# Two selective scans in a four-layer network: step sizes summed on TensorE, softplus in halves, one owned state per half

## The chip, the cores and the metric

The program runs on 1 core of one Trainium2 chip. The metric is the device time of one execution in microseconds (us). It runs ten stages one after the other, with a barrier between them; two of them are the stages that the change touches.

## The reference, cut to what matters

Layers 0 and 3 begin with a Mamba block (a selective scan) whose input is the context and whose gate is the normalised stream. Per batch element (4 of them, 512 time steps, 512 channels, 16 states):

```python
u = silu(conv(in_proj_w @ ctx) + conv_b)
x_dbl = x_proj_w @ u                       # 16 rows of dt_lo, 16 of B, 16 of C
delta = softplus(dt_proj_w @ dt_lo + dt_proj_b)
A = -exp(A_log)
# for each time step t, channel e, state n
state = state * exp(delta * A) + (delta * u) * B_t
y_t = sum_n state * C_t
y = (y + D * u) * silu(z)
```

The other stages (a quantised feed-forward, attentions, two ternary feed-forwards, a routed attention) are the same before and after.

## The kernel before, in words

`stage_mamba` (L294 to L853) is called twice: for layer 0 (stage A here, in the trace from about 60 to 608 us) and for layer 3 (stage B, about 3184 to 3692 us). Channels lie on partitions in EB = 4 blocks of 128, time along the free axis. The work of a batch is NU = 32 units, numbered k = 0 to 31: units 0 to 15 are the 16 states for the first two channel blocks (the first half), units 16 to 31 the same for the other two. A unit n is, across the engines:

- SyncE loads the rows of B and C for the state, spread over 128 partitions (`rows_of`, L416, 5 buffers).
- ScalarE makes two decay tiles dA = exp(delta * A) (L701). There are NA = 3 PSUM banks for them, so it can be at most three tiles, one and a half units, ahead of the scans.
- GpSimd makes dB = du * B for both blocks in one instruction (L733, 4 buffers), and two units later the product of the second block's states with C (L715, `product(n - 2)`).
- VectorE scans the first block (L794), scans the second (L803), and makes the first block's product with C (L811). In an owned unit (`OWN = (5, 12)`, L336, so k = 5, 12, 21, 28) VectorE makes the second product too (L817) and GpSimd skips it.
- TensorE adds both products to y through an identity matrix (L553, L561), a 128x512 matmul in float32 each. The product buffers are 4 deep, so a scan waits for the add of four units before.

Between the units the engines work on the next batch, at places written out by hand (L364 to L372; ScalarE's are three units later, LAG): TensorE's projection (k = 0 to 3), convolution (k = 7 to 10), the small projection (13) and the step sizes (16 to 19); ScalarE's copies, its gates (four silu instructions at k = 10, beside two of the four silu of u; the other two at 13) and Abs and Relu of the step sizes (19 to 22). Stage A also prepares the first batch of stage B, and leaves u, delta and du in DRAM for it (L444), so its four batches all carry such work; of stage B's four batches the last carries none. So there are seven full batches and one bare batch. In stage A's third batch and stage B's first, VectorE also builds the diagonal matrices of layer 3.

Softplus is computed as relu(x) + log(1 + exp(-|x|)) + a correction of the rounding of 1 + exp. Before, over whole 128x2048 tiles:

1. k = 23: ScalarE takes Exp (L655); k = 24: Ln (L659).
2. k = 24: VectorE makes the correction, L765 (two adds of constants) and L766 (a subtraction) (`log_error`).
3. k = 26: GpSimd adds the correction to the logarithm (L709, `add_error`), ahead of its unit's dB.
4. k = 28: VectorE adds the relu (L771) and multiplies by u (L774) (`softplus`), ahead of its unit's scans.

The work on the next batch uses two PSUM banks in turn (`bank`, L403); TensorE waits in `free_bank` until the result that lay in the bank two items before was read.

Of the kernel before, what the change touches and what calls it, by code (L numbers as in the profile page):

```python
# [293 lines left out]
def stage_mamba(chip, name, bc_dram, weights, then=None, given=None):  # L294
# [10 lines left out]
    with ExitStack() as st:  # L305
# [30 lines left out]
        OWN = (5, 12)  # L336
# [18 lines left out]
        s_c, s_err, s_log, s_del, s_du = sem("dve_chain"), sem("log_error"), sem("log"), sem("delta"), sem("du")  # L355
# [10 lines left out]
        SILU, EXP, LOG, ERROR, ADD_ERROR, DELTA = (10, 13), 23, 24, 24, 26, 28  # L366
        LAG = 3
        ROOT, INVERSE = 5, 7

        REWEIGH = {(0, 1): (0, 1), (0, 2): (2, 3)} if given else {(2, 22 + i): (i,) for i in range(4)} if then else {}  # L370
# [7 lines left out]
        if not given:  # L378
            ITEMS += [("project", 0, e) for e in range(EB)] + [("conv", 0, e) for e in range(EB)]
            ITEMS += [("xdbl", 0, 0)] + [("step", 0, e) for e in range(EB)]  # L380
        BEFORE = len(ITEMS)
        AT = {}
        for b in range(B):
            for k in range(NU):
# [4 lines left out]
                if b + 1 < NB:  # L389
                    if k in project_at(b):  # L390
                        here.append(("project", b + 1, project_at(b).index(k)))
                    if k in CONV:
                        here.append(("conv", b + 1, CONV.index(k)))
                    if k == XDBL:
                        here.append(("xdbl", b + 1, 0))
                    if k in STEP:
                        here.append(("step", b + 1, STEP.index(k)))
                AT[b, k] = here
# [8 lines left out]
        def _(sp):  # L407
# [29 lines left out]
            for b in range(NB):  # L437
# [4 lines left out]
                if b == B:  # L442
                    sp.wait_ge(s_du, NB)
# [27 lines left out]
        def _(pe):  # L471
            if given:
                for sem_, count in ((s_x, EB), (s_conv, EB), (s_dbl, 1), (s_dt, EB)):
# [4 lines left out]
            def free_bank(n):  # L478
# [108 lines left out]
        def _(act):  # L587
            act.wait_ge(weights.s_small, weights.SMALL)
            act.activation(a_neg[:], a_in[:], ACT.Exp).then_inc(s_a, 1)
            if given:  # L590
                for sem_, count in ((s_xin, EB), (s_u, EB), (s_dblc, 1), (s_ab, EB), (s_relu, EB), (s_e, 1), (s_ln, 1)):
# [18 lines left out]
            def copy_in(b, e):  # L610
                act.wait_ge(s_x, b * EB + e + 1)
                if b:
                    act.wait_ge(s_err, b)
# [3 lines left out]
            def silu(b, e):  # L617
# [3 lines left out]
                if b >= 2:  # L621
                    act.wait_ge(s_du, b - 1)
# [4 lines left out]
            def gates(b):  # L627
# [3 lines left out]
                for e in range(EB):  # L631
# [11 lines left out]
            def step(b, e):  # L643
                act.wait_ge(s_dt, b * EB + e + 1)
                if b:
                    act.wait_ge(s_del, b)
# [5 lines left out]
            def exp_part(b):  # L652
                act.wait_ge(s_ab, (b + 1) * EB)
                act.wait_ge(s_conv, (b + 1) * EB)
                act.activation(xin[:, :, TAPS - 1:], delta[b % 2][:], ACT.Exp, scale=-1.0).then_inc(s_e, 1)  # L655

            def log_part(b):
                act.wait_ge(s_e, b + 1)
                act.activation(delta[b % 2][:], xin[:, :, TAPS - 1:], ACT.Ln, bias=1.0).then_inc(s_ln, 1)  # L659

            if not given:
# [7 lines left out]
                exp_part(0)  # L669
                log_part(0)  # L670
                norm.root(act)
            for b in range(B):
                act.wait_ge(s_del, b + 1)
                for k in range(NU):
# [4 lines left out]
                    if k == SILU[0]:  # L679
                        gates(b)  # L680
                    for i in REWEIGH.get((b, k - REWEIGH_LAG), ()):
                        reweigh(b, i)
                    if b + 1 < NB:
# [9 lines left out]
                        if k == EXP:  # L693
                            exp_part(b + 1)
                        if k == LOG:
                            log_part(b + 1)
# [8 lines left out]
        def _(pool):  # L705
            def add_error(b):
                pool.wait_ge(s_ln, b + 1)
                pool.wait_ge(s_err, b + 1)
                pool.tensor_tensor(delta[b % 2][:], delta[b % 2][:], du[b % 2][:], ALU.add).then_inc(s_log, 1)  # L709

# [6 lines left out]
            if given:  # L717
                pool.sem_inc(s_log, 1)
            else:
                add_error(0)  # L720
            for b in range(B):
                for k in range(NU):
                    if b + 1 < NB:
                        if k == ADD_ERROR:
                            add_error(b + 1)
                    n, h = b * NU + k, k // N
                    pool.wait_ge(s_du, b + 1)
# [13 lines left out]
        def _(dve):  # L741
# [14 lines left out]
            if given:  # L756
                for sem_ in (s_err, s_del, s_du):
                    dve.sem_inc(sem_, 1)
# [3 lines left out]
            def log_error(b):  # L762
                ex, t = xin[:, :, TAPS - 1:], du[b % 2]
                dve.wait_ge(s_e, b + 1)
                ch.step(dve.tensor_scalar(t[:], ex, 1.0, -1.0, ALU.add, ALU.add))  # L765
                dve.tensor_tensor(t[:], ex, t[:], ALU.subtract).then_inc(s_err, 1)  # L766
# [52 lines left out]
            if not given:  # L819
                log_error(0)  # L820
                norm.inverse(dve)
                softplus(0)
            for b in range(B):
                for k in range(NU):
# [11 lines left out]
                    if b + 1 < NB:  # L836
                        if k == ERROR:
                            log_error(b + 1)
                        if k == DELTA:
                            softplus(b + 1)  # L840
# [2229 lines left out]
```

## Time and profile before

| | |
|---|---|
| median of 3 runs | 4228.2 us (4226.68 to 4228.35) |
| profiled execution | 4224.04 us, of which the traced span 4222.2 us |
| busy over the span: TensorE / VectorE / ScalarE / GpSimd | 85% / 70% / 42% / 36% |
| VectorE's first scan of the first batch, stage A | starts at 90.36 us |
| last gated product's last add, stage A | ends at 607.6 us |
| VectorE's first scan of the first batch, stage B | starts at 3195.66 us |
| last add, stage B | ends at 3692.0 us |

Shares over the whole span say little here, since the stages have different limits. The two stages in question take about 1045 us of the 4222 us. They are read batch by batch, and within one batch unit by unit. In the rows below L-numbers are lines of the kernel before; "idle before" in square brackets is how long the engine had been idle when the instruction started, and what it waited for. Start-to-start distances of the same instruction are what a unit costs; single durations overlap by about 0.1 us. A float32 matmul shows as two records.

### The profile page before, as it was taken

How to read it: one execution, taken by the hardware profiler on the slowest of the kernel's cores; microseconds unless marked ns; L12 is line 12 of the kernel's file. 1: busy time of each engine (PE TensorE's matmuls, PEld its weight loads, DVE VectorE, ACT ScalarE, POOL GpSimd, SP SyncE). 2: the span in 40 equal slices, each digit the busy share in tenths (PEclk: the TensorE clock that was granted, in tenths of full speed). 3: DMA queues.
4: the chain of work that ended last, by engine and by line, in shares of the span. 5: the costliest groups of instructions: out<-in, count | busy, mean ns of one | idle time of the engine just before them, and what ended most of it. 6: DMA issues, size and time to landing. Idle time of an engine off the chain costs nothing. (4 is left out here: it accounts for less than half of the span.)

```text
span 4222.2 us, 46653 instructions
## 1 busy us (share of the span) xinstructions
PE 3601.3 (85%) x15115; PEld 1721.6 (41%) x15163; DVE 2957.5 (70%) x4169; ACT 1763.2 (42%) x2945; POOL 1503.5 (36%) x1038
## 2 busy tenths in 40 slices
PE   5788764999999999898999879785877887689898
PEld 2233322555555555442333344333333332244454
DVE  4889988588777884457888266527667899844663
ACT  3555541222222221243777453327664555421254
POOL 2999863122211220054000100004436999800122
PEclk7899887999999999997999989896998888889999
DMA  3455441121333212366774110001005455412420
GB/s 106 131 144 140 122 139 54 49 80 59 94 101 99 73 34 76 116 144 99 80 79 49 53 60 0 3 8 65 0 0 143 135 138 133 127 47 69 79 54 22
DMA packets 249831, 338.33 MB, mean 80 GB/s; under 512 B 45603, under 2 KB 147523, under 8 KB 248037
## 3 DMA queue, kind: packets, MB, share of 16 engines
q1 hardware_dynamic: 249620, 335.70, 32.0%
q8 instruction: 110, 1.80, 0.2%
q14 instruction: 101, 0.82, 0.1%
HBM read 284.38 MB, written 53.35 MB: 80 GB/s over the span
## 5 line engine op out<-in xcount | busy, mean ns | idle before, releaser
L701 ACT ACTIVATE m_dA<-m_delta,m_a_neg 128x512 f32<-128x512 f32 x512 | 349.9, 689 | 473.3 <-DVE m_H_bank L794 386.5
L553 PE MATMUL m_y<-m_H,ident 128*128 128x512 f32 x512 | 307.3, 689 | 180.0 <-DVE m_H L811 179.9
L1899 DVE TENSOR_REDUCE a_core_minus_max<-a_core_a 128x1 f32<-128x512 f32 x512 | 317.1, 683 | 57.6 <-PE a_core_a L1725 57.6
L733 POOL TENSOR_TENSOR m_dB<-m_du,m_BC 128x1024 f32<-128x1024 f32 x128 | 315.6, 2466 | 44.5 <-DMA m_BC<-bc_ready 33.3
L561 PE MATMUL m_y<-m_H,ident 128*128 128x512 f32 x512 | 298.3, 674 | 34.7 <-POOL m_H L715 34.7
L715 POOL TENSOR_TENSOR m_H<-m_H,m_BC 128x512 f32<-128x512 f32 x224 | 300.1, 1340 | 45.3 <-DVE m_H L803 45.2
L1851 ACT ACTIVATE X<-a_core_s 128x512 f32<-128x512 f32 x512 | 264.6, 603 | 93.1 <-PE a_core_s L1725 93.0
L733 POOL TENSOR_TENSOR XN<-m_du,m_BC 128x1024 f32<-128x1024 f32 x128 | 300.9, 2356 | 2.7 <-DMA m_BC<-bc_ready 2.7
L1291 POOL TENSOR_TENSOR ctxT<-ctxT,f_scales 128x1024 f32<-128x1024 f32 x48 | 105.9, 2206 | 532.8 <-DVE ctxT L1116 532.8
L1357 DVE SCALAR_TENSOR_TENSOR XN<-f_u,f_power_back,XN 128x512 f32<-128x512 f32 x128 | 95.8, 748 | 232.2 <-PE f_u L1188 232.2
L1251 ACT ACTIVATE XN<-f_g,f_power_back 128x512 f32<-128x512 f32 x128 | 88.0, 687 | 404.2 <-PE f_g L1188 404.2
L553 PEld LDWEIGHTS m_y<-m_H,ident 128*128 128x128 f32 x512 | 98.0, 212 | 366.8 <-DVE m_H L811 311.4
L1262 ACT CAST f_inter_high<-XN 128x512 fp32r<-128x512 f32 x128 | 79.5, 621 | 384.5 <-DVE XN L1357 384.5
L1725 PE MATMUL a_core_a<-a_core_k,a_core_q 96*128 96x512 bf16 x512 | 209.2, 411 | 23.6 <-ACT a_core_max_rows L1869 10.1
L1178 PE MATMUL f_acc<-f_wdown_high,f_inter_high 128*128 128x512 f32 x512 | 224.1, 438 | 0.0
L1299 POOL TENSOR_TENSOR XN<-f_mag,ctxT 128x1024 f32<-128x1024 f32 x48 | 127.9, 2664 | 213.4 <-DVE f_mag L1125 107.4
L1180 PE MATMUL f_acc<-f_wdown_high,f_inter_low 128*128 128x512 f32 x512 | 202.7, 396 | 0.0
L1179 PE MATMUL f_acc<-f_wdown_low,f_inter_high 128*128 128x512 f32 x512 | 202.2, 395 | 0.0
L1186 PE MATMUL f_g<-f_xn_high,f_wh 128*128 128x512 f16 x512 | 196.5, 384 | 1.4 <-ACT f_wh L1164 1.4
L1725 PE MATMUL a_core_s<-a_core_q,a_core_k 98*128 98x512 bf16 x512 | 192.0, 386 | 6.0 <-ACT X L1851 4.5
L794 DVE TENSOR_TENSOR_SCAN m_H_bank<-m_dA,XN 128x512 f32<-128x512 f32 x128 | 157.4, 1230 | 56.2 <-ACT m_dA L701 36.6
L1186 PE MATMUL f_u<-f_xn_high,f_wh 128*128 128x512 f16 x512 | 195.0, 381 | 1.4 <-ACT f_wh L1164 1.4
(411 smaller groups left out, 8352.7 us busy)
## 6 DMA issues: line engine op xcount, KB each, us to landing
m_BC<-bc_rows SPq DMA_DIRECT2D x224, 512.0 KB, 4.8
XN<-in_L_ffn_w_dram SPq DMA_DIRECT2D x72, 256.0 KB, 2.7
m_BC<-bc_ready SPq DMA_DIRECT2D x32, 512.0 KB, 5.0
ternary<-ctxT SPq DMA_DIRECT2D x96, 128.0 KB, 1.7
a_core_q<-a_q_parts SPq DMA_DIRECT2D x48, 256.0 KB, 12.8
a_core_k<-a_k_parts SPq DMA_DIRECT2D x48, 256.0 KB, 14.6
f_w_tern<-ternary SPq DMA_DIRECT2D x24, 512.0 KB, 5.9
f_core_q<-f_q_parts SPq DMA_DIRECT2D x24, 512.0 KB, 8.2
```

The lines of the kernel that those rows point to most:

```text
L553: pe.matmul(ps_y[:, 0, :], ident[:], HD[n % NH], start=False, stop=True, skip_group_check=True).then_inc(s_ad, 1)
L561: pe.matmul(ps_y[:, 1, :], ident[:], HP[n % NH], start=False, stop=True, skip_group_check=True).then_inc(s_ap, 1)
L701: act.activation(dA[:, i % NA, :], delta[b % 2][:, e, :], ACT.Exp, scale=a_neg[:, e, k % N:k % N + 1]).then_inc(s_dA, 1)
L715: pool.tensor_tensor(HP[n % NH], HP[n % NH], BC[n % NS][:, 1, :], ALU.mult).then_inc(s_hp, 1)
L733: pool.tensor_tensor(dB[n % ND][:], du[b % 2][:, h * EH:(h + 1) * EH, :], BC[n % NS][:, 0:1, :].broadcast_to([P, EH, L]), ALU.mult).then_i ...
L1178: pe.matmul(ps_acc[:, t, :], high, DH[gb][:, q % 4, :], start=(q % 4 == 0), stop=False)
L1179: pe.matmul(ps_acc[:, t, :], high, DL[gb][:, q % 4, :], start=False, stop=False)
L1180: m = pe.matmul(ps_acc[:, t, :], low, DH[gb][:, q % 4, :], start=False, stop=(q % 4 == 3))
L1186: pe.matmul(out, w[0], xh[:, k, toks], start=(k == 0), stop=False)
L1725: pe_last = pe.matmul(out[:, cols], lhs(c, k), rhs(c, k), start=(c == 0), stop=(c == NCH - 1 and mask is None))
L1851: act.activation(prob[pair][e][:, j, q0:], ps_s[:, at % NR, q0:], ACT.Exp, scale=hs.scale).then_inc(s_exp, 1)
L1899: dve.tensor_reduce(mx[u % 2][:, qt, h:h + 1], ps_a[:, at % NR, 0:n], AX.X, ALU.max, negate=True).then_inc(s_red, 1)
```

## The change

- Softplus goes through in two halves of two channel blocks. Exp of the first half on ScalarE at k = 21, of the second at 22; Ln at 22 and 23. VectorE's correction (the same two instructions, on 128x1024) at k = 22 and 24.
- `add_error` on GpSimd and `softplus` on VectorE go. TensorE sums the three terms of each block through the identity matrix into a PSUM bank (new item "sum", three float32 matmuls of 128x512, at k = 23, 24, 26, 27).
- Two units later VectorE multiplies the block's sum, read from PSUM, by u (`times_u`, four 128x512 instructions at k = 25, 26, 28, 29). Four units after the sum ScalarE copies it to delta (`copy_sum`, four 128x512 copies at k = 27, 28, 30, 31), after `times_u` of the block.
- The gates are split: two at k = 10 and two at k = 13.
- `OWN = (9,)`: one state per half, so k = 9 and 25, is finished by VectorE alone, where there were two.
- The turning of layer 3's weights in stage A moves from k = 22 to 25 to k = 20, 21, 22, 25. GpSimd waits per half for du. In stage A the parking of u, delta and du waits for the last copy.

```diff
-        OWN = (5, 12)
+        OWN = (9,)
...
-        SILU, EXP, LOG, ERROR, ADD_ERROR, DELTA = (10, 13), 23, 24, 24, 26, 28
-        LAG = 3
+        SILU, EXP, LOG, ERROR, SUM = (10, 13), (21, 22), (22, 23), (22, 24), (23, 24, 26, 27)
+        LAG, TIMES_U, COPY_SUM = 3, 2, 4
...
+                elif kind == "sum":
+                    pe.wait_ge(s_del, b * EB + i + 1)
+                    pe.wait_ge(s_du, b * EB + i + 1)
...
+                elif kind == "sum":
+                    pe.wait_ge(s_relu, b * EB + i + 1)
+                    pe.wait_ge(s_ln, 2 * b + i // EH + 1)
+                    pe.wait_ge(s_err, 2 * b + i // EH + 1)
+                    pe.matmul(out, ident[:], delta[b % 2][:, i, :], start=True, stop=False)
+                    pe.matmul(out, ident[:], du[b % 2][:, i, :], start=False, stop=False)
+                    pe.matmul(out, ident[:], positive[:, i, :], start=False, stop=True).then_inc(s_sum, 1)
...
-            def gates(b):
+            def gates(b, h):
...
-                for e in range(EB):
+                for e in range(h * EH, (h + 1) * EH):
...
+            def exp_part(b, h):
+                rows = slice(h * EH, (h + 1) * EH)
+                act.wait_ge(s_ab, b * EB + (h + 1) * EH)
...
+            def log_part(b, h):
+                rows = slice(h * EH, (h + 1) * EH)
+                act.wait_ge(s_e, 2 * b + h + 1)
...
+            def copy_sum(b, e):
+                act.wait_ge(s_sum, b * EB + e + 1)
+                act.wait_ge(s_du, b * EB + e + 1)
+                act.copy(delta[b % 2][:, e, :], bank("sum", b, e)).then_inc(s_del, 1)
...
-            def add_error(b):
-                pool.wait_ge(s_ln, b + 1)
-                pool.wait_ge(s_err, b + 1)
-                pool.tensor_tensor(delta[b % 2][:], delta[b % 2][:], du[b % 2][:], ALU.add).then_inc(s_log, 1)
...
-                    pool.wait_ge(s_du, b + 1)
+                    pool.wait_ge(s_du, b * EB + (h + 1) * EH)
...
-            def softplus(b):
-                dve.wait_ge(s_log, b + 1)
-                dve.wait_ge(s_relu, (b + 1) * EB)
-                dve.tensor_tensor(delta[b % 2][:], delta[b % 2][:], positive, ALU.add).then_inc(s_del, 1)
-                dve.wait_ge(s_del, b + 1)
-                dve.wait_ge(s_u, (b + 1) * EB)
-                dve.tensor_tensor(du[b % 2][:], delta[b % 2][:], u[b % 2][:], ALU.mult).then_inc(s_du, 1)
+            def log_error(b, h):
+                rows = slice(h * EH, (h + 1) * EH)
+                ex, t = xin[:, rows, TAPS - 1:], du[b % 2][:, rows, :]
+                dve.wait_ge(s_e, 2 * b + h + 1)
+                ch.step(dve.tensor_scalar(t, ex, 1.0, -1.0, ALU.add, ALU.add))
+                dve.tensor_tensor(t, ex, t, ALU.subtract).then_inc(s_err, 1)
+
+            def times_u(b, e):
+                dve.wait_ge(s_sum, b * EB + e + 1)
+                dve.wait_ge(s_u, b * EB + e + 1)
+                dve.tensor_tensor(du[b % 2][:, e, :], bank("sum", b, e), u[b % 2][:, e, :], ALU.mult).then_inc(s_du, 1)
```

## Rows read from the trace of the kernel before

**Rows 1.** Busy time by batch, stage B's third and fourth (columns as in the header).

```profile
core 0: us, PE busy (x) PEld busy (x) DVE busy (x) ACT busy (x) POOL busy (x), PEclk, DMA share, GB/s
3453.10:3576.20 123.10, 102.70 (x217) 40.09 (x218) 112.24 (x113) 67.21 (x93) 117.06 (x62) 0.89 0.50 137
3576.20:3685.00 108.80, 76.04 (x153) 28.40 (x153) 101.16 (x108) 47.53 (x67) 105.94 (x60) 0.91 0.53 141
```

**Rows 2.** VectorE in order of time, first scans of k = 10, 18 to 23.

```profile
3491.31 1.23 DVE L794 TENSOR_TENSOR_SCAN m_H_bank<-m_dA,XN 128x512 f32<-128x512 f32 x1 [4.31 <-ACT m_dA L701]
...
3518.28 1.23 DVE L794 TENSOR_TENSOR_SCAN m_H_bank<-m_dA,XN 128x512 f32<-128x512 f32 x1 [0.20 <-DVE m_H L811]
...
3521.71 1.22 DVE L794 TENSOR_TENSOR_SCAN m_H_bank<-m_dA,XN 128x512 f32<-128x512 f32 x1
...
3524.83 1.23 DVE L794 TENSOR_TENSOR_SCAN m_H_bank<-m_dA,m_dB 128x512 f32<-128x512 f32 x1 [0.20 <-DVE m_H L811]
...
3527.95 1.23 DVE L794 TENSOR_TENSOR_SCAN m_H_bank<-m_dA,m_dB 128x512 f32<-128x512 f32 x1 [0.20 <-DVE m_H L811]
...
3532.10 1.23 DVE L794 TENSOR_TENSOR_SCAN m_H_bank<-m_dA,XN 128x512 f32<-128x512 f32 x1
...
3535.22 1.23 DVE L794 TENSOR_TENSOR_SCAN m_H_bank<-m_dA,XN 128x512 f32<-128x512 f32 x1 [0.20 <-POOL m_dB L733]
```

**Rows 3.** VectorE in order of time, k = 24 to 28, around the correction and softplus.

```profile
3541.04 2.29 DVE L766 TENSOR_TENSOR m_du<-m_xin,m_du 128x2048 f32<-128x2048 f32 x1
3543.25 1.22 DVE L794 TENSOR_TENSOR_SCAN m_H_bank<-m_dA,m_dB 128x512 f32<-128x512 f32 x1
...
3550.31 1.23 DVE L794 TENSOR_TENSOR_SCAN m_H_bank<-m_dA,XN 128x512 f32<-128x512 f32 x1 [1.03 <-POOL XN L733]
...
3553.84 1.23 DVE L794 TENSOR_TENSOR_SCAN m_H_bank<-m_dA,XN 128x512 f32<-128x512 f32 x1 [0.61 <-POOL XN L733]
...
3559.53 3.24 DVE L774 TENSOR_TENSOR m_du<-m_delta,m_u 128x2048 f32<-128x2048 f32 x1
3562.69 1.22 DVE L794 TENSOR_TENSOR_SCAN m_H_bank<-m_dA,m_dB 128x512 f32<-128x512 f32 x1
```

**Rows 4.** The correction's first instruction by line: ns min/median/max, first and last start.

```profile
L765 DVE TENSOR_SCALAR m_du<-m_xin x8: 1218/2794/2978, 75.0 to 3538.1; 128x2048 f32<-128x2048 f32 x8
```

**Rows 5.** GpSimd in order of time, same batch.

```profile
3523.41 2.37 POOL L733 TENSOR_TENSOR m_dB<-m_du,m_BC 128x1024 f32<-128x1024 f32 x1
...
3530.49 2.36 POOL L733 TENSOR_TENSOR XN<-m_du,m_BC 128x1024 f32<-128x1024 f32 x1
3532.80 2.35 POOL L733 TENSOR_TENSOR m_dB<-m_du,m_BC 128x1024 f32<-128x1024 f32 x1
...
3538.64 1.27 POOL L715 TENSOR_TENSOR m_H<-m_H,m_BC 128x512 f32<-128x512 f32 x1
3543.47 4.50 POOL L709 TENSOR_TENSOR m_delta<-m_delta,m_du 128x2048 f32<-128x2048 f32 x1 [3.55 <-DVE m_du L766]
...
3557.29 3.32 POOL L715 TENSOR_TENSOR m_H<-m_H,m_BC 128x512 f32<-128x512 f32 x1
3560.58 4.39 POOL L733 TENSOR_TENSOR m_dB<-m_du,m_BC 128x1024 f32<-128x1024 f32 x1
```

**Rows 6.** ScalarE in order of time, same batch, at k = 10 and 24.

```profile
3484.23 2.93 ACT L633 ACTIVATE XN<-X,m_norm_shift,m_norm_rstd 128x512 f32<-128x512 f32 x4
...
3488.53 0.69 ACT L624 ACTIVATE m_u<-m_w,m_small 128x512 f32<-128x512 f32 x1 [0.80 <-PE m_w L524]
...
3534.07 1.28 ACT L659 ACT_TABLE_LOAD   x1
3535.37 1.91 ACT L659 ACTIVATE m_delta<-m_xin 128x2048 f32<-128x2048 f32 x1
```

**Rows 7.** TensorE in order of time, same batch, around the convolution (L524).

```profile
3477.09 1.24 PE L553 MATMUL m_y<-m_H,ident 128*128 128x512 f32 x2 [2.12 <-DVE m_H L811]
3478.12 5.22 PE L524 MATMUL m_w<-m_xin,m_taps 128*128 128x512 f32 x8
...
3484.90 3.60 PE L524 MATMUL m_w<-m_xin,m_taps 128*128 128x512 f32 x8
```

More of the change, by code:

```diff
@@ L365, in stage_mamba @@
         PROJECT, TURN, CONV, XDBL, STEP = (0, 1, 2, 3), (5, 6, 11, 12), (7, 8, 9, 10), 13, (16, 17, 18, 19)
-        SILU, EXP, LOG, ERROR, ADD_ERROR, DELTA = (10, 13), 23, 24, 24, 26, 28
-        LAG = 3
+        SILU, EXP, LOG, ERROR, SUM = (10, 13), (21, 22), (22, 23), (22, 24), (23, 24, 26, 27)
+        LAG, TIMES_U, COPY_SUM = 3, 2, 4
         ROOT, INVERSE = 5, 7
-        REWEIGH = {(0, 1): (0, 1), (0, 2): (2, 3)} if given else {(2, 22 + i): (i,) for i in range(4)} if then else {}
+        REWEIGH = {(0, 1): (0, 1), (0, 2): (2, 3)} if given else {(2, k): (i,) for i, k in enumerate((20, 21, 22, 25))} if then else {}
         REWEIGH_LAG = 1 if given else 3
@@ L379, in stage_mamba @@
             ITEMS += [("project", 0, e) for e in range(EB)] + [("conv", 0, e) for e in range(EB)]
-            ITEMS += [("xdbl", 0, 0)] + [("step", 0, e) for e in range(EB)]
+            ITEMS += [("xdbl", 0, 0)] + [("step", 0, e) for e in range(EB)] + [("sum", 0, e) for e in range(EB)]
         BEFORE = len(ITEMS)
@@ L397, in stage_mamba @@
                         here.append(("step", b + 1, STEP.index(k)))
+                    if k in SUM:
+                        here.append(("sum", b + 1, SUM.index(k)))
                 AT[b, k] = here
@@ L472, in _ @@
             if given:
-                for sem_, count in ((s_x, EB), (s_conv, EB), (s_dbl, 1), (s_dt, EB)):
+                for sem_, count in ((s_x, EB), (s_conv, EB), (s_dbl, 1), (s_dt, EB), (s_sum, EB)):
                     pe.sem_inc(sem_, count)
@@ L668, in _ @@
                     step(0, e)
-                exp_part(0)
-                log_part(0)
+                for h in range(2):
+                    exp_part(0, h)
+                for h in range(2):
+                    log_part(0, h)
                 norm.root(act)
+                for e in range(EB):
+                    copy_sum(0, e)
             for b in range(B):
-                act.wait_ge(s_del, b + 1)
+                act.wait_ge(s_del, (b + 1) * EB)
                 for k in range(NU):
@@ L678, in _ @@
                         act.wait_ge(s_given[k // N], 32)
-                    if k == SILU[0]:
-                        gates(b)
+                    if k in SILU:
+                        gates(b, SILU.index(k))
                     for i in REWEIGH.get((b, k - REWEIGH_LAG), ()):
@@ L692, in _ @@
                             step(b + 1, STEP.index(k - LAG))
[L693 to L696, printed above, removed]
+                        if k in EXP:
+                            exp_part(b + 1, EXP.index(k))
+                        if k in LOG:
+                            log_part(b + 1, LOG.index(k))
+                        if k - COPY_SUM in SUM:
+                            copy_sum(b + 1, SUM.index(k - COPY_SUM))
                     for j in range(EH):
@@ L819, in _ @@
             if not given:
-                log_error(0)
+                for h in range(2):
+                    log_error(0, h)
                 norm.inverse(dve)
-                softplus(0)
+                for e in range(EB):
+                    times_u(0, e)
             for b in range(B):
@@ L836, in _ @@
                     if b + 1 < NB:
[L837 to L840, printed above, removed]
+                        if k in ERROR:
+                            log_error(b + 1, ERROR.index(k))
+                        if k - TIMES_U in SUM:
+                            times_u(b + 1, SUM.index(k - TIMES_U))
                     n = b * NU + k
```

37 lines of the change are left out of this document (11 added, 26 removed).

## Prediction

> **What bounds the kernel now.** I read the two scan stages alone; nothing else is touched. First the busy time by batch [rows 1]: of the 123.1 us of a full batch VectorE is busy 112.2, GpSimd 117.1, TensorE 102.7 (granted clock 0.89 on average). All three are near full, so the next view has to be the order of time. The reader should measure there from first scan to first scan. A plain unit costs VectorE 3.12 us (3521.71 to 3524.83), a unit with one gated product ahead 3.43, so such an extra costs 0.31; an owned unit costs 4.15 (3527.95 to 3532.10) [rows 2]. GpSimd needs 3.54 for a plain unit (two from 3523.41 to 3530.49) and 2.31 for an owned one, since it skips the product [rows 5]. Over 32 units with four owned, VectorE's part is 28 x 3.12 + 4 x 4.15 = 104.0, GpSimd's 28 x 3.54 + 4 x 2.31 = 108.4. VectorE then carries, per full batch, the correction, 8.03 - 3.12 = 4.9 (3535.22 to 3543.25) [rows 2, 3]; softplus, 8.85 - 3.12 = 5.7 (3553.84 to 3562.69); waits of 1.03 + 0.61 for GpSimd right ahead of it [rows 3]; a wait of 4.31 for ScalarE at k = 10 [rows 2]; and eight gated or added products, 8 x 0.31 = 2.5. Each wait replaces a gap of 0.2 that a plain unit has anyway. 104.0 + 4.9 + 5.7 + 1.2 + 4.1 + 2.5 = 122.4 of 123.1: the chain of VectorE explains the batch. GpSimd's 117.1 are inflated: the two operations of softplus stretch its product from 1.27 to 3.32 and its dB from 2.35 to 4.39, and it adds the correction itself, 4.50 after an idle 3.55 [rows 5].
>
> **Part by part, for one full batch.**
>
> *Softplus* goes from VectorE: -5.7. In its place four products that read PSUM, 128x512, of the kind of a gated product: 4 x 0.31 = +1.2. Bounds: +0 (all in existing gaps) to +3.5 (0.68 of work and 0.2 of gap each).
>
> *Owned units* four to two: -2 x (4.15 - 3.12) = -2.1.
>
> *GpSimd's add* goes, and with it VectorE's two waits: -(1.03 + 0.61 - 0.4) = -1.2. GpSimd takes on two products. Its need becomes 30 x 3.54 + 2 x 2.31 = 110.8, plus the time in which VectorE's correction holds it, taken at that correction's free duration, 1.22 + 2.29 = 3.5 [rows 3, 4]: 114.3. That is a floor for a full batch.
>
> *The correction in halves.* L765 takes 1.22 at its fastest, when GpSimd rests, and 2.79 in the median; the one of this batch ran while GpSimd finished a dB and the product of 3538.64, and then L766 took 2.29 unhindered because GpSimd sat idle 3.55 waiting for it [rows 3 to 5]. After the change GpSimd doesn't wait for the correction but goes on, so L766 meets it too, and there are four shorter operations to meet it. Free, the four cost 3.5, less two gaps of 0.28: 3.1. If each waits for a whole dB, 3.1 + 4 x 2.35 = 12.5. I take about 1.1 us of waiting for each, near half of a GpSimd instruction (2.35 or 1.27): 3.1 + 4.4 = 7.5, so +2.6 against 4.9; bounds -1.8 to +7.6.
>
> The Trainium skill (SBUF — State Buffer, "Who interferes with whom") says that a VectorE instruction with two SBUF inputs, or one in a two-port mode, and a GpSimd instruction that reads SBUF exclude each other for the whole instruction, and that whoever issues later blocks. The stretched rows above agree; it speaks for the PSUM operand and against the halves.
>
> *ScalarE at k = 22 and 23.* A switch of function costs a table load of 1.28 [rows 6]; Exp and Ln in halves at different k make four loads where there were two, +2.6. ScalarE's lead is 1.5 units, about 3.75 us, less its two decay tiles. At k = 22 it has Relu and Abs (two like L624's 0.69), Exp and Ln of half the 1.91 of L659 each, and two loads: 5.8 [rows 6]; at k = 23 Ln and two loads, 3.5. The correction's first half on VectorE (3 to 4 us) covers the first, the second half at k = 24 comes too late for the second. I add 0.6 of stall; bounds 0 and 3.5.
>
> The Trainium skill (ScalarE: Activation LUTs, "What ACT_TABLE_LOAD costs") gives 2.66 us for a switch, load and drain together. Here Ln starts 0.02 after the end of its load, so this trace shows 1.28 alone [rows 6].
>
> *Gates split.* At k = 10 ScalarE did two loads, four gates (2.93), two silu: 7.1 us, and waited 0.80 for TensorE's convolution on top [rows 6]; VectorE lost 4.31. Now k = 10 carries 5.5, under cover of the owned unit 9, which adds 1.03 to the lead: stall 0.5 to 1.5. k = 13 carries 5.5 too instead of 3.9, no longer behind an owned unit 12: 5.5 - 3.75 - 0.3 = 1.5. So 2.5 in place of 4.1 (3.2 in stage A): -1.3 on average, bounds -3.5 and +1. The convolution helps: it took 5.22 for the first block at the low clock level (1.2 GHz) after an idle 2.12 that the owned unit 5 had left TensorE, against 3.60 at the high level (2.4 GHz) [rows 7], and unit 5 is no longer owned.
>
> *TensorE* gets 12 matmuls. A convolution block's four take 3.60 at the high level, the last one's tail among it [rows 7], so 0.86 each, 10.3 in all. Its need at that level, 64 adds and 36 other matmuls at 0.86 and 16 transposes of a quarter of that, is 89; with the sums 99 of about 117 us. `times_u` sits two units behind its sum: from the product of unit 22 to k = 25 lie two units and a half correction, about 9 us, against 2.6 for the sum (5.1 at the low level) and 1.7 for two adds. The reuse of a bank waits for `copy_sum`, which ScalarE reaches 1.5 units ahead of VectorE, so before TensorE comes for it; queued behind that wait are the adds, whose buffers are 4 deep. I put +0.5 for it, bounds 0 and +4. The four copies on ScalarE (at most 0.69 each, as L624) hide in its idle time: it is busy 67.2 of 123.1 [rows 1].
>
> *Sum*: -5.7 + 1.2 - 2.1 - 1.2 + 2.6 + 0.6 - 1.3 + 0.5 = -5.4, giving 117.7, above the floor of 114.3. Seven full batches: -38. The bare batch loses two owned units (-2.1) and most of its stall at k = 10, but takes 108.8 now [rows 1] and GpSimd needs 110.8 less a lead of at most 3.5: -1. Before the first batch of stage A the serial chain of the correction, GpSimd's 4.5, and two operations of 2.29 gives way to two sums, a product and copies that end at nearly the same time: -0.8, bounds -3 and +3. At the end of stage A the parking starts some 6 us later, and had 9 us to spare: 0. Layer 3's turning between the sums makes TensorE wait for a copy at k = 25 once: +0.5. Together -39: 4224.0 - 39 = 4185 in the profiled execution. The median of the runs lies 4.2 above that execution; I keep the distance: **4189 us**.
>
> **The rivals.**
>
> *GpSimd sets the pace.* If the corrections hardly meet GpSimd and ScalarE is covered, VectorE's chain falls to about 113 and the floor of 114.3 decides: -8.8 a batch, 7 x 8.8 + 1 = 63, so 4166. For it: GpSimd's 3.54 against 3.12. Against: the measured median of L765.
>
> *The four corrections wait in full.* They cost 12.5 instead of 7.5, the batch falls by 0.4 to 2: 4228 less 3 to 15, about 4218. For it: L765's median, 2.79 against 1.22. Against: the next GpSimd instruction has to be ready each time.
>
> *The table switch costs what the page says.* By the Trainium skill's 2.66 the two more loads cost 2.8 more a batch: 4208. Against: the row above.
>
> *Slower: TensorE at the low clock level.* The sums come exactly where VectorE pauses for the corrections and TensorE idles. From k = 23 to 31 TensorE has 9 x 1.71 + 10.3 = 25.7 us of work at the high level, 51.4 at the low one; VectorE needs 8 x 3.12 + 4.15 + 1.2 + 4.1 = 34.4 and bears a lag of some 3.2. All at the low level costs 51.4 - 37.6 = 13.8 a batch, net +8.4, 59 in all: 4287. It decides from about two thirds of these matmuls at the low level on, where the cost reaches 5.4. For it: the drop in rows 7 after an idle of only 2.12. Against: the second block's 3.60 right behind shows the high level back within some 5 us of steady work, and the sums are steady work.
>
> *It does not do what it says*: the work comes off VectorE but every place it frees is filled by ScalarE's and TensorE's waits: within 8 us of 4228.
>
> **How the numbers follow.** The forecast, 4176 to 4206, 0.58; GpSimd's pace 0.12; full waits of the corrections 0.13, the table switch 0.02; no effect 0.06; TensorE slower 0.09. About 0.2% (8.5 us) is what a measurement can tell. Faster: 0.58 + 0.12 + 0.02 + most of 0.13 = 0.83; same 0.08; slower 0.09. The range leaves out the slower case, half of no effect, and the far end of GpSimd's pace: 4167 to 4222.
>
> **What would show it.** VectorE's pitch over k = 25 to 31 stays 3.12 plus 0.31 where a product with u stands; a wait for TensorE's sum there would break the softplus step. GpSimd's instructions above 3 us vanish, those beside the corrections remain. The halves of L765 and L766 sum to about 7.9 a batch. VectorE's waits for ScalarE are 0.5 to 1.5 at k = 10 and 1.5 at k = 13. TensorE's granted clock from k = 22 to 28 stays mostly high. The prediction is wrong if the batch takes over 121 or under 114 us.

## The result and the profile after

The changed kernel takes 4213.3 us (median of 15 runs) against 4222.7 us for the kernel before (15 runs); the ratio is 0.998, with a 95% interval from 0.9972 to 0.9987. So it is faster by about 9 us, where 39 were forecast. The fifteen runs of the kernel before have a median 5.5 us below that of the three runs from which the forecast started. The time lies inside the range, but the range reached to within a microsecond of 4222.7, so that says little. The profiled execution took 4212.0 us against 4224.0, its span 4210.3 against 4222.2.

Where the 12 us of the span lie, by the first scans of the batches: the start of the first stage costs 3.5 us more (first scan at 93.88 against 90.36 us), stage A's 127 units from first to last first scan take 12.8 us less, stage B's 4.3 us less, and the other stages differ by 1.6. Batch by batch (before, after, in us): stage A 128.7 / 124.1, 123.7 / 123.6, 135.4 / 131.0; stage B 134.4 / 135.7, 123.1 / 121.0, 123.1 / 121.0. The last batch of a stage has no next one to measure to; from its first to its last first scan it is 119.4 / 115.6 in stage A and, the bare batch, 105.8 / 104.4 in stage B. The forecast had wanted 5.4 from each full batch.

Busy time of stage B's third and fourth batch in the changed kernel, which answers to [rows 1] (columns as in its header):

```profile
core 0: us, PE busy (x) PEld busy (x) DVE busy (x) ACT busy (x) POOL busy (x), PEclk, DMA share, GB/s
3442.80:3563.80 121.00, 105.01 (x241) 42.52 (x242) 113.88 (x115) 71.89 (x101) 111.41 (x63) 0.96 0.53 140
3563.80:3671.30 107.50, 75.57 (x153) 25.58 (x154) 99.49 (x106) 50.04 (x69) 107.49 (x62) 0.95 0.53 141
```

GpSimd is down from 117.1 to 111.4, near the need of 110.8 that was forecast, and TensorE's clock is up from 0.89 to 0.96. But VectorE, from which softplus and two owned units had gone (7.8 us by the prediction's terms, with 1.2 us of products coming in), is busy 113.9 of 121.0, 1.6 more than before. The order of time shows on what. VectorE in the third batch of stage B, from the correction ahead of k = 22 to the first product with u, ahead of k = 25, which answers to [rows 3] (L780 and L781 are the correction, L786 the products with u, L806 the first scans):

```profile
3518.12 6.26 DVE L780 TENSOR_SCALAR m_du<-m_xin 128x1024 f32<-128x1024 f32 x1
3524.42 1.23 DVE L781 TENSOR_TENSOR m_du<-m_xin,m_du 128x1024 f32<-128x1024 f32 x1
3525.56 1.23 DVE L806 TENSOR_TENSOR_SCAN m_H_bank<-m_dA,XN 128x512 f32<-128x512 f32 x1
...
3528.67 1.23 DVE L806 TENSOR_TENSOR_SCAN m_H_bank<-m_dA,XN 128x512 f32<-128x512 f32 x1 [0.20 <-ACT m_dA L727]
...
3531.51 1.81 DVE L780 TENSOR_SCALAR m_du<-m_xin 128x1024 f32<-128x1024 f32 x1
3533.35 3.25 DVE L781 TENSOR_TENSOR m_du<-m_xin,m_du 128x1024 f32<-128x1024 f32 x1
3536.53 1.22 DVE L806 TENSOR_TENSOR_SCAN m_H_bank<-m_dA,m_dB 128x512 f32<-128x512 f32 x1
...
3539.36 0.67 DVE L786 TENSOR_TENSOR m_du<-m_w,m_u 128x512 f32<-128x512 f32 x1
```

An instruction with 0.68 us of work (what it takes in stage A's third batch, beside an idle GpSimd) is recorded for 6.26: the recorded time includes a wait. GpSimd at the same time:

```profile
3517.93 2.38 POOL L747 TENSOR_TENSOR XN<-m_du,m_BC 128x1024 f32<-128x1024 f32 x1
3520.23 1.29 POOL L736 TENSOR_TENSOR m_H<-m_H,m_BC 128x512 f32<-128x512 f32 x1
3521.46 2.38 POOL L747 TENSOR_TENSOR m_dB<-m_du,m_BC 128x1024 f32<-128x1024 f32 x1
3527.97 1.27 POOL L736 TENSOR_TENSOR m_H<-m_H,m_BC 128x512 f32<-128x512 f32 x1 [4.13 <-DVE m_H L815]
3529.20 2.34 POOL L747 TENSOR_TENSOR m_dB<-m_du,m_BC 128x1024 f32<-128x1024 f32 x1
3531.51 1.25 POOL L736 TENSOR_TENSOR m_H<-m_H,m_BC 128x512 f32<-128x512 f32 x1
3532.73 2.79 POOL L747 TENSOR_TENSOR XN<-m_du,m_BC 128x1024 f32<-128x1024 f32 x1
```

GpSimd goes through three instructions at full pace, the one in progress when L780 comes (3517.93) and two that begin after it. The third ends at 3523.84; L780 ends 0.54 later, about the time it needs. GpSimd had by then run out of work: its next product waits for a scan that stands behind L780 on VectorE. So VectorE waited until GpSimd was waiting for VectorE. Six of the seven full batches show this (L780 between 6.16 and 7.25), always ended by GpSimd running dry; in the seventh, stage A's third, GpSimd was idle and it took 0.68. At the second half the instruction got in one instruction later (1.81), then L781 waited out a dB (3.25, of which 1.23 is work). Five of the seven second halves are alike to 0.02 us; stage A's third and fourth are cheaper (1.39 and 3.25; 0.68 and 2.17).

### The profile page after: what moved, and what is told of

Its sections match the earlier page's. It is cut to its first block and busy times, and to the rows that moved or that the text cites. A ratio compares the mean times of both kernels' runs of the same rounds, so it can differ in the third digit from the quotient of the medians.

```text
span 4210.3 us, 47286 instructions
## 1 busy us (share of the span) xinstructions
PE 3635.0 (86%) x15355; PEld 1743.4 (41%) x15355; DVE 2959.2 (70%) x4185; ACT 1801.8 (43%) x3009; POOL 1463.2 (35%) x1046
## 5 line engine op out<-in xcount | busy, mean ns | idle before, releaser
L566 PE MATMUL m_y<-m_H,ident 128*128 128x512 f32 x512 | 283.3, 641 | 150.0 <-DVE m_H L823 149.6
L747 POOL TENSOR_TENSOR m_dB<-m_du,m_BC 128x1024 f32<-128x1024 f32 x128 | 302.0, 2360 | 123.0 <-DVE m_du L786 84.5
L574 PE MATMUL m_y<-m_H,ident 128*128 128x512 f32 x512 | 268.4, 612 | 12.0 <-POOL m_H L736 11.9
L1201 PE MATMUL f_u<-f_xn_low,f_wh 128*128 128x512 f16 x512 | 194.8, 380 | 0.0
## 6 DMA issues: line engine op xcount, KB each, us to landing
a_core_q<-a_q_parts SPq DMA_DIRECT2D x48, 256.0 KB, 12.8
```

Source lines behind the costliest of these rows:

```text
L566: pe.matmul(ps_y[:, 0, :], ident[:], HD[n % NH], start=False, stop=True, skip_group_check=True).then_inc(s_ad, 1)
L574: pe.matmul(ps_y[:, 1, :], ident[:], HP[n % NH], start=False, stop=True, skip_group_check=True).then_inc(s_ap, 1)
L747: pool.tensor_tensor(dB[n % ND][:], du[b % 2][:, h * EH:(h + 1) * EH, :], BC[n % NS][:, 0:1, :].broadcast_to([P, EH, L]), ALU.mult).then_i ...
```

## The experiments

"Starves" below means: the VectorE instruction is held through the GpSimd instruction in progress and through others that begin after it. Unless said otherwise the pitches given are of stage B's third batch: "unit k" from its first scan to the next one, with the correction that lies between. So the corrections ahead of k = 22 and 24 lie in units 21 and 23.

**1. The add of constants left out.**

```diff
-                ch.step(dve.tensor_scalar(t, ex, 1.0, -1.0, ALU.add, ALU.add))
-                dve.tensor_tensor(t, ex, t, ALU.subtract).then_inc(s_err, 1)
+                dve.tensor_tensor(t, ex, ex, ALU.subtract).then_inc(s_err, 1)
```

> The changed kernel without the first instruction of each half's correction (the adds of +1 and -1, L780); the second subtracts the exponential from itself, so the rounding correction is left out. Theory (the single-source add starves while GpSimd issues back to back; the two-source subtract gets in at the next boundary): the unit before the first correction falls from 10.28 to 3.12 + at most 2.35 + 1.23 = 6.7 us, the second from 7.86 to about 5.5 to 6.7; a full batch falls from 121.0 by 3 to 6 us, all runs by 20 to 40 us. Rival (the 6.3 us are a wait of VectorE for ScalarE's Exp or a queue behind it, not for GpSimd): the subtract takes over the 6.3 us and the batch falls by at most 1 us.

The result of this kernel lacks the rounding correction. 4189.3 us, 0.992 of the kernel before (0.9904 to 0.9937), batch 117.5. The saving came, but not by the theory. VectorE in this kernel, the first and the second half's remaining instruction:

```profile
3500.07 6.80 DVE L780 TENSOR_TENSOR m_du<-m_xin 128x1024 f32<-128x1024 f32 x1
...
3512.74 2.34 DVE L780 TENSOR_TENSOR m_du<-m_xin 128x1024 f32<-128x1024 f32 x1
```

The two-input instruction starves just as long: 5.57 us of wait and 1.23 of work. The rival's number for the subtract was right, but its cause wasn't: GpSimd's third instruction ends at 3505.78, again where the wait ends. Of the 3.5 us that the batch saves, 2.0 are the second half's second wait and 1.4 the two adds' own work.

**2. No correction at all.**

```diff
-                ch.step(dve.tensor_scalar(t, ex, 1.0, -1.0, ALU.add, ALU.add))
-                dve.tensor_tensor(t, ex, t, ALU.subtract).then_inc(s_err, 1)
+                dve.sem_inc(s_err, 1)
...
-                    pe.matmul(out, ident[:], du[b % 2][:, i, :], start=False, stop=False)
```

> The changed kernel with no correction at all: VectorE's L780 and L781 and TensorE's middle matmul of each sum are left out, so delta lacks the rounding correction. Theory: VectorE loses 11.9 us a full batch, so its chain would be 109.1 us, below GpSimd's 30 x 3.54 + 2 x 2.31 = 110.8 us; the batch lands at 110.8 to 112.5 us and VectorE shows waits of 0.6 us for GpSimd in many units. Time about 4213 - 7 x 9.3 = 4148 us. Rival (TensorE or ScalarE hold the batch): it stays above 116 us.

4157.7 us, 0.9846 (0.9829 to 0.9862), batch 113.5. The correction costs the changed kernel 56 us, 7.5 a batch. The wait that now comes last is not GpSimd's, as I had expected, but ScalarE's: 2.71 at k = 22 and 2.06 at k = 23. There ScalarE changes four times between Ln and the Exp of the decay tiles, a table load each time, and in the changed kernel these loads lay hidden behind the starving instruction. Run 8 tests that.

**3. The add written with two inputs**, to tell whether the kind of instruction decides.

```diff
-                ch.step(dve.tensor_scalar(t, ex, 1.0, -1.0, ALU.add, ALU.add))
+                ones = minus_one[:].rearrange("p (a o) -> p a o", a=1).broadcast_to([P, EH, L])
+                ch.step(dve.scalar_tensor_tensor(out=t, in0=ex, scalar=1.0, in1=ones, op0=ALU.add, op1=ALU.add))
```

> Same arithmetic as the changed kernel, but the first correction instruction is written with two SBUF inputs (exponential + 1, then plus a tile of -1) instead of one. It takes 1.2 us free instead of 0.68. Theory: a two-source instruction gets in at the next GpSimd boundary, so each takes at most 2.35 + 1.2 = 3.6 us, and L780's 6.3 us of the first half fall to 2.5 to 3.6; the second half's rise from 1.8 by up to 1 us. A full batch falls by 1 to 4 us, the kernel by 7 to 28 us. Rival (both kinds starve alike): L780 stays at 6 us or more in the first half, and the kernel becomes 0 to 8 us slower.

The tile `minus_one` is filled once at the start. 4221.8 us, 0.9997 (0.9987 to 1.0006): what the rival said, and 8.6 us slower than the changed kernel. All instances of the line (min, median, max in ns, first and last start):

```profile
L783 DVE SCALAR_TENSOR_TENSOR m_du<-m_xin,m_minus_one x16: 1214/2344/6997, 74.5 to 3541.8; 128x1024 f32<-128x1024 f32 x16
```

In the first half six of the seven wait 4.6 to 5.8 us. The number of inputs does not decide; my theory of the single-source form fell with runs 1 and 3.

**4. GpSimd rests during both corrections.** The arithmetic is unchanged, and nothing but two waits is added.

```diff
+                    if b + 1 < NB and k == ERROR[0] + 1:
+                        pool.wait_ge(s_err, 2 * (b + 1) + 1)
                     pool.wait_ge(s_du, b * EB + (h + 1) * EH)
...
+                    if b + 1 < NB and k == ERROR[1] + 1:
+                        pool.wait_ge(s_err, 2 * (b + 1) + 2)
                     if n >= 2:
                         product(n - 2)
```

> The changed kernel with two waits on GpSimd: at k = 23 its dB waits for the first half's correction, and at k = 25 its product waits for the second half's. GpSimd then rests while VectorE corrects. Theory: the first correction takes 0.7 + 1.2 us (10.28 becomes 5.0 us), the second 0.1 to 0.8 + 1.2 us (7.86 becomes about 5.2 us); GpSimd loses some 2 us twice and its need is 110.8 + 4 = 115 us; a full batch 115 to 117 us, the kernel 4213 - 7 x 5 = 4178 us (4170 to 4190). Rival (the long add is no contention): nothing on VectorE shrinks, and GpSimd's rest costs up to 4 us a batch: 4213 to 4240 us.

4178.4 us, 0.9893 (0.9877 to 0.991), batch 115.7. VectorE from k = 22 to 24 in this kernel (L784 and L785 are the correction, L810 the first scans):

```profile
3493.61 0.68 DVE L784 TENSOR_SCALAR m_du<-m_xin 128x1024 f32<-128x1024 f32 x1
3494.33 1.23 DVE L785 TENSOR_TENSOR m_du<-m_xin,m_du 128x1024 f32<-128x1024 f32 x1
3496.40 1.23 DVE L810 TENSOR_TENSOR_SCAN m_H_bank<-m_dA,XN 128x512 f32<-128x512 f32 x1 [0.85 <-ACT m_dA L727]
...
3501.39 1.23 DVE L810 TENSOR_TENSOR_SCAN m_H_bank<-m_dA,XN 128x512 f32<-128x512 f32 x1 [2.07 <-ACT m_dA L727]
...
3504.23 1.37 DVE L784 TENSOR_SCALAR m_du<-m_xin 128x1024 f32<-128x1024 f32 x1
3505.63 1.23 DVE L785 TENSOR_TENSOR m_du<-m_xin,m_du 128x1024 f32<-128x1024 f32 x1
```

This settles the cause: with GpSimd held back the same four instructions take 4.5 us in place of 12.5 (L784's 1.37 still waits for the rest of one dB), and added waits make the kernel 35 us faster than the changed one. Of the 8.0 us a batch 2.7 go to ScalarE, whose table loads come to light as in run 2.

**5. Two owned states per half again.**

```diff
-        OWN = (9,)
+        OWN = (5, 12)
```

> The changed kernel with two owned states per half again (k = 5, 12, 21, 28). What the single owned state is worth. If VectorE's chain sets the batch: +2.1 us a full batch, and 0 to +1 in the batches that GpSimd paces, so about +12 to +15 us on 4213. If GpSimd sets it: faster, by up to 2.5 us a batch. A side effect that the theory of a GpSimd backlog expects: with unit 21 owned, GpSimd skips the product that stands in the row of three instructions in front of the first correction, so the correction's 6.3 us fall by about 1.3 us and the net is about +5 us.

Median 4215.4 us, 0.9986 (0.9976 to 0.9995). The batch is 1.7 us longer than the changed kernel's (122.7): the owned units 5 and 12 cost 2.1, the wait ahead of k = 10 is back at 4.31 although the gates stay split (net +1.7 there, since unit 9 is plain), unit 21 with the correction gets 1.35 cheaper although it is now owned, and the rest is small waits, 0.4 more in unit 4 and 1.0 less in unit 12. The side effect expected of a backlog is there: with the product of unit 21 skipped, it is held through two GpSimd instructions instead of three, and L780 takes 3.47 instead of 6.26. The profiled execution, 4223.9, is 12 us above the changed kernel's, but it is the slowest of ten runs that scatter from 4212 to 4224; their median is only 2 us above, and the two intervals overlap. So the wait and the held instruction are shown by the trace, and a slower kernel is not shown.

**6. All four gates at k = 10.**

```diff
-                    if k in SILU:
-                        gates(b, SILU.index(k))
+                    if k == SILU[0]:
+                        gates(b, 0)
+                        gates(b, 1)
```

> The changed kernel with all four gates at k = 10 again. Forecast's working: the stall of VectorE ahead of k = 10 grows from 1.5 to 3.0 to 3.5 us, the one at k = 13 (0.3 now) vanishes: net +1.3 to +1.8 us a full batch, +9 to +13 us. Rival (the convolution on TensorE, not the gates, decides when ScalarE is free): within 3 us of 4213.

4214.6 us, 0.9976 (0.9967 to 0.9986), batch 121.1: no difference, the rival. The wait at k = 10 grows from 1.52 to 2.30, unit 12, which lost 0.98 to an add on TensorE and 0.30 to ScalarE, gets 1.2 cheaper, and the first correction waits 0.5 longer. The split of the gates moves a wait and brings nothing; most of what shortened the wait of 4.31 was the owned unit 9, since with units 5 and 12 owned the split alone left it at 4.31 (run 5).

**7. The correction in one piece at k = 23.** The halves are undone on VectorE alone (the call ahead of the first batch, not shown, likewise).

```diff
-        ... ERROR, SUM = ..., (22, 24), (23, 24, 26, 27)
+        ... ERROR, SUM = ..., (23,), (23, 24, 26, 27)
...
-                ex, t = xin[:, rows, TAPS - 1:], du[b % 2][:, rows, :]
-                dve.wait_ge(s_e, 2 * b + h + 1)
+                ex, t = xin[:, :, TAPS - 1:], du[b % 2][:]
+                dve.wait_ge(s_e, 2 * b + 2)
...
-                dve.tensor_tensor(t, ex, t, ALU.subtract).then_inc(s_err, 1)
+                dve.tensor_tensor(t, ex, t, ALU.subtract).then_inc(s_err, 2)
```

> The changed kernel, but the correction is made in one piece of 2048 columns at k = 23 in place of two of 1024 at k = 22 and 24; everything else stays in halves. Free it costs 1.2 + 2.3 us. Theory (the cost is in how often VectorE has to win the shared port from a busy GpSimd, and the first try waits until GpSimd has run out of work): one such wait in place of two, about 5.6 + 3.5 = 9.1 us or, if the port is won at a boundary, 1.1 + 3.5 + 1 = 5.6 us, against 11.9 us now: a batch shorter by 2.8 to 6 us, 4170 to 4195 us. Rival (it costs what its columns cost): 11.9 us as now, 4213 us.

4195.8 us, 0.9938 (0.992 to 0.9956), batch 118.6. The add takes 4.62, of which 1.22 is work, and the subtract 2.29 without a wait, 6.9 in all against 12.5: one lost wait instead of three. Of the 5.6 us saved the batch keeps 2.4; most of the rest goes to ScalarE, whose 2.71 at k = 22 shows here too.

**8. The two rests of run 4, and both Ln parts behind one table load.**

```diff
-                        if k in LOG:
-                            log_part(b + 1, LOG.index(k))
+                        if k == LOG[1]:
+                            log_part(b + 1, 0)
+                            log_part(b + 1, 1)
```

> The kernel in which GpSimd rests during the corrections (4178), with both Ln parts at k = 23 behind one table load, so two loads fewer a batch. There VectorE waited for ScalarE 0.85 us at k = 22 and 2.07 us at k = 23. Theory (these waits are the table loads): they fall to 0 and about 1 us, a batch shorter by 1.5 to 2.5 us, 4178 - 7 x 2 = 4164 us, unless GpSimd's need of about 115 us a batch takes their place (then 4174). Rival (TensorE holds it): no change, 4178.

4170.9 us, 0.9871 (0.9853 to 0.9889), batch 114.2, 1.5 less than in run 4, and ScalarE's waits at k = 22 and 23 are gone, 2.7 us. 1.2 of them go back to the corrections, which now wait 0.98 and 0.94 for GpSimd and take 5.7 in place of 4.5. VectorE also waits 0.61 for GpSimd ahead of k = 9, and units 7 and 8 take GpSimd's 3.53 and 3.54: its pace is reached there.

**9. Only the first rest.**

```diff
+                    if b + 1 < NB and k == ERROR[0] + 1:
+                        pool.wait_ge(s_err, 2 * (b + 1) + 1)
```

> The changed kernel with only the first of the two rests: GpSimd's dB at k = 23 waits for the first half's correction; the second correction meets a busy GpSimd as before. Theory: the first correction's unit falls from 10.28 to about 5.6 us (with ScalarE's wait of 0.85 showing), then 2.1 us of waiting for ScalarE at k = 23, the second's unit stays at 7 to 7.9 us. A batch 118 us, the kernel about 4213 - 7 x 2.8 = 4193 us. Rival (the two rests only work together, or the first merely moves the loss to the second): 4205 to 4213 us.

4187.1 us, 0.9921 (0.9904 to 0.9937), batch 117.1. The first rest brings 26 us, the second another 9.

**10. Run 8, and the start of stage A by halves** (the edits of run 8 aren't repeated).

```diff
-                for e in range(EB):
+                for e in range(EH):
                     copy_sum(0, e)
             for b in range(B):
-                act.wait_ge(s_del, (b + 1) * EB)
                 for k in range(NU):
+                    if not given and b == 0 and k in (1, 2):
+                        copy_sum(0, EH + k - 1)
+                    if k % N == 0:
+                        act.wait_ge(s_del, b * EB + (k // N + 1) * EH)
```

> GpSimd rests during both corrections, both Ln parts stand behind one table load (4171 so far), and the start of the first scan stage is split by halves: ScalarE copies two sums before the first decay tiles and the other two at k = 1 and 2, and waits for delta per half. Theory: the first scan, at 93.88 us in the changed kernel and 90.36 before, starts after the second copy (86.6), the table load and one decay tile, so at about 89 to 90 us: 4 to 5 us less, 4166 us. Rival (the two late copies come between ScalarE's tiles or hold TensorE's banks, and the first units pay it back): 4170 us.

4166.0 us, 0.9868 (0.9852 to 0.9885). The first scan starts at 90.02 us, not 94.36 as in run 8. This is the fastest kernel that computes everything: about 47 us below the changed kernel and 57 below the one before. Its third batch in stage B:

```profile
3399.30:3513.50 114.20, 104.12 (x241) 42.47 (x242) 107.16 (x115) 68.95 (x99) 112.31 (x63) 0.99 0.53 148
```

**11. The kernel before with one owned state per half**, one part of the change alone.

```diff
-        OWN = (5, 12)
+        OWN = (9,)
```

> The kernel before with one part of the change alone: one owned state per half, k = 9 and 25. Forecast's working: -2.1 us of owned units and about -1.8 to -2.8 us of the wait of 4.31 at k = 10, which now lies behind an owned unit: a full batch 123.05 - 4.4 = 118.7 us, the kernel 4222 - 30 = 4192 us. Rival (GpSimd, which has two more products and still its add of 4.5 us and the two stretched instructions, sets the batch: 110.8 + 4.5 + 3.6 + 4.1 = 123 us): no change, 4218 to 4225 us, with waits for GpSimd of 0.6 us in many units.

4215.0 us, 0.9982 (0.9972 to 0.9991); the batch is 123.2, not shorter at all. Up to unit 21 the owned units and the wait at k = 10 are cheaper by 3.8 us, near what was worked out; then the correction's unit takes 3.5 more (11.54 for 8.03) and softplus's 1.1. VectorE at k = 24 and GpSimd beside it:

```profile
3529.53 6.46 DVE L765 TENSOR_SCALAR m_du<-m_xin 128x2048 f32<-128x2048 f32 x1
3536.03 2.29 DVE L766 TENSOR_TENSOR m_du<-m_xin,m_du 128x2048 f32<-128x2048 f32 x1
```

```profile
3527.80 2.36 POOL L733 TENSOR_TENSOR m_dB<-m_du,m_BC 128x1024 f32<-128x1024 f32 x1
3530.11 1.28 POOL L715 TENSOR_TENSOR m_H<-m_H,m_BC 128x512 f32<-128x512 f32 x1
3531.34 2.35 POOL L733 TENSOR_TENSOR m_dB<-m_du,m_BC 128x1024 f32<-128x1024 f32 x1
3533.64 1.27 POOL L715 TENSOR_TENSOR m_H<-m_H,m_BC 128x512 f32<-128x512 f32 x1
3538.47 4.50 POOL L709 TENSOR_TENSOR m_delta<-m_delta,m_du 128x2048 f32<-128x2048 f32 x1 [3.55 <-DVE m_du L766]
```

The whole tile starves as the half does, until GpSimd's own add waits for it. It is held through the rest of a dB and three more instructions. In the kernel before, with the extra owned units taking products off GpSimd, it was held through the rest of a dB and one product and took 2.95. So starvation needs no halves. At the first try it lasts as long as GpSimd has instructions ready: the one in progress and one more in run 5, two more in the changed kernel, three more here.

## Why the prediction was wrong

The direction was right; the size was about four times too large. Term by term, for stage B's third batch:

- *Softplus off VectorE* (-5.7 + 1.2): right. A unit with a product with u costs 3.43, as any gated product's does, and none waited for TensorE there. All 32 of these products, which read one operand from PSUM, took 0.67 to 0.69 us; none was held up by GpSimd.
- *Owned units* (-2.1): right, 4.20 beyond the product with u at k = 25.
- *GpSimd's add and the waits for it* (-1.2): right, both waits are gone and GpSimd has no instruction above 3 us in this batch.
- *Gates and k = 10* (-1.3): the size is right, the reason is not. 4.1 us became 1.4 ahead of k = 10 and 1.5 in unit 12, together 1.3 less. Runs 5 and 6 show that the owned unit 9 did most of it and not the split, and of the 1.3 lost in unit 12, 0.98 is a wait for an add on TensorE.
- *The correction in halves* (+2.6, bounds -1.8 to +7.6): **this is the step that failed.** Units 21 and 23 with the corrections cost 10.28 and 7.86, so 11.9 above two plain units; the old one cost 4.9. The term is +7.0. I had let each of four instructions wait half of a GpSimd instruction. They waited 5.6, 0, 1.1 and 2.0. The upper end had allowed each a whole dB, 9.4 together, and the sum of 8.7 lies under it, but the way there was not in the prediction: one instruction can be held through three in a row. The prediction saw that GpSimd would no longer pause for the correction and that L766's unhindered 2.29 rested on the idle 3.55 [rows 3, 5], and then priced the loss of that pause at a mean wait. It had also read in its own rows that L765 was held through the rest of a dB and through the product of 3538.64, which began 0.6 us after it; that is one instruction let past already, and the price of half an instruction did not use it. Over the seven full batches units 21 and 23 grew by 40 us, 47 without the 7.2 that unit 21 saves by no longer being owned; 18 were forecast. That excess, 29 us, is about the whole miss, 27 us on the profiled executions.
- *ScalarE at k = 22 and 23* (+0.6): 0 in the changed kernel, but only under cover of the starving instruction. Uncovered it is 2.7 (run 4) or 4.4 (run 2) above the usual gaps, where I had 0.6 and an upper bound of 3.5. Had the corrections cost what I said, this term would probably have been short by some 2 us; no run has them at that cost.
- *TensorE* (+0.5): nothing at the sums and copies that I had priced. The 0.98 in unit 12 is counted above. Its clock did fall, as the slower case had it. TensorE, third batch of stage B, the add that was held up and the first two matmuls of a sum:

```profile
3528.53 2.07 PE L566 MATMUL m_y<-m_H,ident 128*128 128x512 f32 x2 [8.29 <-DVE m_H L823]
3530.39 1.91 PE L544 MATMUL m_w<-m_delta,ident 128*128 128x512 f32 x2
3532.10 1.31 PE L545 MATMUL m_w<-m_du,ident 128*128 128x512 f32 x2
```

By the granted clock, in stretches of 4 us around it:

```profile
3522.00:3526.00 4.00, 0.00 (x0) 0.00 (x0) 3.97 (x3) 3.76 (x4) 1.83 (x1) 0.55 0.54 140
3526.00:3530.00 4.00, 1.47 (x2) 0.83 (x3) 3.80 (x5) 1.44 (x3) 2.03 (x2) 0.50 0.00 1
3530.00:3534.00 4.00, 4.00 (x7) 1.57 (x6) 3.96 (x4) 1.32 (x2) 4.00 (x3) 0.67 0.49 137
3534.00:3538.00 4.00, 4.00 (x11) 1.74 (x10) 4.00 (x3) 0.22 (x1) 1.52 (x1) 1.00 0.49 127
```

  After the 8.29 us idle it ran at the low level (1.2 GHz) for one add and a matmul and a half and then at the high one (2.4 GHz). The products with u stand two units behind, and none of them waited. Where nothing starves the clock is 0.99 over the whole batch (run 10), against 0.96.

Sum for that batch: -5.7 + 1.2 - 2.1 - 1.2 + 7.0 - 1.3 = -2.1, as measured. Stage A's first, third and fourth batch did better (4.6, 4.4 and 3.8 us). In the first 2.75 of it is none of the forecast's terms: the wait for GpSimd ahead of the next batch's first scan fell from 4.87 to 2.12. In the third GpSimd was idle at the first correction. Three places did worse:

- The start of stage A (-0.8 forecast, +3.5 measured). I had two sums on the path; ScalarE waits for delta as a whole, so it is four sums, the first of them at the low clock level (2.05, 1.92 and 1.21 for its matmuls), the others 2.57 apart on a TensorE without a gap, and the last one's product and copy and the table load come behind them. Run 10 takes it back. It lay outside the bounds I gave by half a microsecond.
- Stage A's second batch (-5.4 forecast, -0.1 measured). Its corrections cost 1.7 more than those of stage B's third batch: L780 took 7.25, the longest, and in the kernel before L765 had taken only 1.22 here. And here the rival "GpSimd sets the pace" holds for nine units: after GpSimd's late first dB (idle 4.58 before it), VectorE has caught up with GpSimd and waits for it in every unit that has no other work, at 3.54 us a unit. Before, the owned unit 5 ended this. First scans of k = 2 to 5:

```profile
225.06 1.23 DVE L806 TENSOR_TENSOR_SCAN m_H_bank<-m_dA,XN 128x512 f32<-128x512 f32 x1 [0.61 <-POOL XN L747]
...
228.60 1.23 DVE L806 TENSOR_TENSOR_SCAN m_H_bank<-m_dA,XN 128x512 f32<-128x512 f32 x1
...
232.13 1.23 DVE L806 TENSOR_TENSOR_SCAN m_H_bank<-m_dA,m_dB 128x512 f32<-128x512 f32 x1 [0.61 <-POOL m_dB L747]
...
235.67 1.23 DVE L806 TENSOR_TENSOR_SCAN m_H_bank<-m_dA,m_dB 128x512 f32<-128x512 f32 x1 [0.62 <-POOL m_dB L747]
```

- Stage B's first batch (+1.2 measured). ScalarE's wait ahead of k = 10 is 3.15, hardly less than the 3.40 before, and the owned unit 9 comes on top. Layer 3's diagonals on VectorE take 0.6 more than before.

Of the rivals, "the four corrections wait in full" comes nearest in time and stood at 0.13; its mechanism, each waiting for one instruction, isn't what happened. The floor of 114.3 us was near: with the waits out of the way the batch settles at 114.2 (runs 8 and 10), of which GpSimd is busy 112.3 in run 10. The sum behind it differs (110.8 and 3.5 of held time), so that it fits to 0.1 us is partly luck.

The Trainium skill (SBUF — State Buffer, "Who interferes with whom") says that the later of the two blocks until the first finishes. The traces agree that the two exclude each other; they differ on how long the later one waits, which was the remainder of one GpSimd instruction and the whole of two more (5.6 us at 3518.12).

## What to carry to other kernels

Before taking work off a companion engine, look at what its pauses were good for: in the kernel before, GpSimd's wait for the correction was what let its second instruction through at its free 2.29 us, and the two further owned units kept short what stood ready ahead of the first. When two engines shut each other out, as VectorE's correction and GpSimd's products do here, and the short instruction sits on the critical one, make the other rest for it with a semaphore; two waits on GpSimd made this kernel 35 us faster than the same work without them. And price a wait for a shared resource by the run of ready instructions on the other side, not by the mean length of one.

## What the runs showed of the hardware that I had not expected

- VectorE's correction, with its operands in SBUF, was held through the one in progress and through those that stood ready behind it (mostly two more in the changed kernel and three in run 11), each at its full pace, and came through when GpSimd ran dry: 5.5 to 6.6 us of wait in the changed kernel, 2.8 to 3.5 with one product fewer ahead (run 5), 4.1 to 5.2 for the whole tile (run 11, six batches). One input or two made no difference (runs 1, 3).
- It is not always so. At the second half VectorE came through after one instruction (1.1 us), and where GpSimd was busy as the subtract came up, the subtract always had the next turn (2.0 of a dB, or 0.94). What decides which turn it gets stays open: neither the kind of the VectorE instruction nor of the GpSimd instruction behind whose end it tried, nor how long the next one had been ready, sorts the cases, and no run was made to tell it apart.
- A table load on ScalarE cost 1.28 us in every switch; where the next activation had nothing else to wait for it began 0.01 to 0.02 us later. Two loads fewer a batch took 2.7 us of ScalarE's waits from VectorE, of which 1.5 reached the batch (run 8).
